# A four-layer graph network on one core: a fourth pair list with six passes behind it, and three smaller edits

## The reference, cut to what matters

```python
def step(f, _):                       # second layer, K = 10, ALPHA = 0.1
    msg = f[src] * edge_weight[:, None]
    agg = segment_sum(msg, dst, num_segments=n)
    return 0.9 * agg + 0.1 * feat_0, None
x = layernorm(x + relu_sum_layer(x, edge_attr, src, dst, eps))      # layer 0
x = layernorm(x + scan(step, x, length=10))                         # layer 1
x = layernorm(x + typed_mlp_layer(x, edge_weight1, w1, w2, src, dst, edge_type))   # layer 2
x = layernorm(x + segment_max_layer(x, theta, phi, src, dst))       # layer 3
```

## Time and profile before

| | |
|---|---|
| median of three runs | 4459.67 us |
| profiled execution, own time | 4465.7 us |
| its span | 4463.9 us |
| mean granted TensorE clock | 0.744 |
| VectorE busy | 2971.8 us (67%) |
| GpSimd busy | 2610.8 us (58%) |
| TensorE busy | 2502.3 us (56%) |

### The profile page before, as it was taken

How to read it: one execution, slowest core, us unless ns; L and a number is a source line. 1 busy time by engine, 2 the same in 40 slices (tenths; PEclk the granted TensorE clock), 3 DMA queues, 4 the chain that set the end, 5 groups by cost and what they waited for, 6 DMA issues and landing times. The chain is left out here.

```text
span 4463.9 us, 60648 instructions
## 1 busy us (share of the span) xinstructions
PE 2502.3 (56%) x9482; PEld 1176.3 (26%) x9482; DVE 2971.8 (67%) x7710; ACT 1232.9 (28%) x3893; POOL 2610.8 (58%) x2544
## 2 busy tenths in 40 slices
PE   4720000677777588888888487561222104995654
PEld 2510000333333244344444222111111101333332
DVE  7989997988888488788888586332332234663333
ACT  0023332332232255445554222111000012441111
POOL 4747772655554477764444564774565613656776
PEclk9965555887777799899999799785555557995555
DMA  6647776888887866675555476333434243332111
GB/s 223 229 119 211 219 217 182 154 152 147 149 149 133 153 173 162 164 164 145 142 142 133 120 208 171 71 57 59 49 49 45 34 99 84 73 68 40 36 37 27
DMA packets 628412, 557.12 MB, mean 125 GB/s; under 512 B 379089, under 2 KB 548122, under 8 KB 623330
## 3 DMA queue, kind: packets, MB, share of 16 engines
q1 hardware_dynamic: 477606, 418.72, 34.7%
q0 software_dynamic: 90112, 95.44, 16.7%
q10 hardware_dynamic: 60612, 42.15, 3.5%
HBM read 291.63 MB, written 290.82 MB: 130 GB/s over the span
## 5 line engine op out<-in xcount | busy, mean ns | idle before, releaser
L1302 POOL DMA_INDIRECT out<-xob,ob x400 | 412.0, 1030 | 358.7 <-DVE xob L1414 251.8
L278 POOL DMA_INDIRECT gb<-nodes,ib x400 | 396.5, 991 | 348.9 <-ACT ib L855 249.6
L491 POOL DMA_INDIRECT xdst<-in_x,dstc x400 | 457.0, 1142 | 226.4 <-issue 135.1
L262 PE MATMUL bank<-ident,act 128*99 128x128 f32 x400 | 84.6, 348 | 666.2 <-DVE act L999 649.4
L298 PE MATMUL bank<-chosen,rec 128*6 128x512 bf16 x1200 | 370.0, 473 | 0.9 <-DVE chosen L285 0.9
L278 POOL DMA_INDIRECT cgb<-layer,ib x160 | 175.6, 1098 | 232.3 <-ACT ib L2193 185.9
L1341 PE MATMUL bank<-hm,w 128*48 128x512 f32 x600 | 296.0, 632 | 0.0
L1358 PE MATMUL bank<-bxT,w 105*128 105x512 f32 x600 | 283.2, 608 | 8.7 <-ACT bxT L1245 8.6
L272 PE MATMUL bank<-ident,scan 99*128 99x99 f32 (+2 forms) x1120 | 199.5, 308 | 152.1 <-DVE scan L2012 101.5
L291 PE MATMUL bank<-l_chosen,l_rec 128*3 128x512 f32 x480 | 250.6, 672 | 0.3 <-DVE l_chosen L285 0.3
L278 POOL DMA_INDIRECT parent<-upper_rows,ib x176 | 176.1, 1000 | 119.1 <-ACT ib L1270 54.6
(11 more groups left out here) (292 smaller groups left out, 6764.8 us busy)
## 6 DMA issues: line engine op xcount, KB each, us to landing
nodes<-wt SPq DMA_DIRECT2D x40, 1286.2 KB
edges<-gb ACTq DMA_DIRECT2D x100, 194.0 KB, 5.9
upper_rows<-tb SPq DMA_DIRECT2D x100, 194.0 KB, 4.9
xa<-upper_rows SPq DMA_DIRECT2D x100, 194.0 KB, 3.0
lsb<-edges SPq DMA_DIRECT2D x100, 194.0 KB
run_rows<-upper_rows SPq DMA_DIRECT2D x100, 194.0 KB, 4.3
deep_sum<-zeros SPq DMA_DIRECT2D x20, 960.0 KB, 21.6
layer<-zeros SPq DMA_DIRECT2D x20, 960.0 KB, 25.1
```

The costliest lines, as they stand in the source:

```text
L262: last = nc.tensor.transpose(slot(dst_ps[0:w, :], t), rows_sb[:, t, c0:c0 + w], ident[:, :])
L278: yield nc.gpsimd.indirect_dma_start(out=dst[s][:, t, 0:width], out_offset=None, in_=table, in_offset=bass.IndirectOffsetOnAxis(ap=ib[s][: ...
L491: nc.gpsimd.indirect_dma_start(out=xdst[:, k * F:(k + 1) * F], out_offset=None, in_=a["x"], in_offset=bass.IndirectOffsetOnAxis(ap=dstc[:, ...
L1302: nc.gpsimd.indirect_dma_start(out=out, out_offset=bass.IndirectOffsetOnAxis(ap=ob[s][:, t:t + 1], axis=0), in_=xo[s][:, t, :], in_offset= ...
```

## The change

`LU` becomes `(4, 4, 2, 2)`, there are 19 rows of `lists`, a third `deep_sum` table and a fourth `list_keep`. Level 2 now also packs a list and scatters its sums, as level 1 does; a new level 3 on the new list does what level 2 did; and `steps` runs on the new list with six passes instead of seven. The norm of list 0 adds the third table. In counting, `hot_no` becomes four 16-bit `tensor_scalar` comparisons, and ScalarE makes one of eight `hot_at` tiles. In the first edge stage the 99 keep rows come from one 1 KB load and one bf16 product of 3 rows, copied by ScalarE from PSUM. The `deep_sum` and `layer` tables are cleared in the second edge stage.

```diff
-LU = (4, 4, 2)
+LU = (4, 4, 2, 2)
...
                 def mark(i, b):                                # counting, ScalarE
+                    nc.scalar.copy(lines[b][:, :], col(line_no, g)).then_inc(s_mark, 1)
                     nc.scalar.copy(marks[b][:, :], col(line_at, g)).then_inc(s_mark, 1)
+                    if b == 1:
+                        nc.scalar.mul(away[:, :], col(line_at, g)[:, T - 1:T], -1.0).then_inc(s_away, 1)
+                        act.wait_ge(s_away, 2 * i + 1)
+                        nc.scalar.activation(gap[:, :], steps_h[:, :], ACT.Abs, bias=away[:, 0:1], scale=1.0).then_inc(s_away, 1)
+                        wait(act, s_count, g - 1)
+                        act.wait_ge(s_away, 2 * i + 2)
+                        nc.scalar.activation(hot_at[b][:, T - 1, :], gap[:, :], ACT.Relu, bias=one[:, 0:1], scale=-1.0).then_inc(s_near, 1)
...
                 def compare(i, b):                             # counting, VectorE
-                    nc.vector.tensor_tensor(hot_no[b][:, :, :], steps_h[:, 0:P]..., col(line_no, g)..., ALU.is_equal)
-                    dve.wait_ge(s_mark, g + 1)
+                    dve.wait_ge(s_mark, 2 * g + 2)
                     for t in range(T):
+                        nc.vector.tensor_scalar(hot_no[b][:, t, :], steps_h[:, 0:P], lines[b][:, t:t + 1], None, ALU.is_equal)
+                    for t in range(T - b):
                         last = nc.vector.tensor_scalar(hot_at[b][:, t, :], steps_h[:, :], marks[b][:, t:t + 1], None, ALU.is_equal)
...
-                for z in (*deep_sum, *layer.values()):         # counting, SP
-                    for j in range(EP * F // P // ZW):
-                        sp.dma_start(zr[:, j * ZW:(j + 1) * ZW], zeros[:, :]).then_inc(s_clear, 16)
...
                 def load(i, s):                                # first edge stage, SP
-                    wait(sp, s_scan, g - U + 1)
-                    sp.dma_start(kb[s][0:2 * F, :], edge_keep[0:1, bass.ds(g * GE, GE)].to_broadcast([2 * F, GE]))
-                    sp.dma_start(kb[s][2 * F:PW, :], edge_keep[0:1, bass.ds(g * GE, GE)])
+                    wait(sp, s_spread, g - U + 1)
+                    sp.dma_start(keeps[s][0:1, :], keep_half[0:1, bass.ds(g * GE, GE)]).then_inc(s_kb[s], 16)
...
+                def copy_keeps(i, s):                          # ScalarE, first in its body, ahead of relued
+                    act.wait_ge(s_spread, g + 1)
+                    wait(act, s_scan, g - U + 1)
+                    nc.scalar.copy(kb[s][:, :], psK[b][0:MW, :]).then_inc(s_kept, 1)
...
+                def spread_keeps(i, s):                        # TensorE, first in its body, ahead of columns
+                    pe.wait_ge(s_kb[s], (i + 1) * 16)
+                    wait(pe, s_kept, g - 1)
+                    nc.tensor.matmul(psK[b][0:MW, :], pick[:, :], keeps[s][:, :], start=True, stop=True).then_inc(s_spread, 1)
...
+                def clear_sums(i, s):                          # second edge stage, SP, listed turns
+                    for z in deep_sum:
+                        sp.dma_start(rows(z, part_of(i) * U + s, 1), blank[:, :]).then_inc(s_blank[s], 16)
+                def clear_layers(i, s):                        # second edge stage, SP, every group
+                    for z in layer.values():
+                        sp.dma_start(rows(z, i * U + s), blank[:, :]).then_inc(s_fresh[s], 16)
...
     level(1, level_rows[0])
     prepare(2, 12, 14)
-    first_rows("deep", (level_rows[2],), (idx3, oi2, w_2))
-    level(2, level_rows[1])
+    level(2, level_rows[1])                                    # with pack_up and scatter to deep_sum[1]
+    prepare(3, 16, 18)
+    first_rows("deep", (level_rows[3],), (idx3, oi2, w_2))
+    level(3, level_rows[2])
...
     one(0, level_rows[3], swap_rows, "first")                  # powers
     one(1, swap_rows, level_rows[3], "add")
-    with eng.Fori(1, (STEPS - 4) // 2) as j:
-        one(j * 2, level_rows[2], swap_rows, "add")
-        one(j * 2 + 1, swap_rows, level_rows[2], "add")
-    one(STEPS - 4, level_rows[2], None, "end")
+    one(2, level_rows[3], swap_rows, "add")
+    one(3, swap_rows, level_rows[3], "add")
+    one(4, level_rows[3], swap_rows, "add")
+    one(STEPS - 5, swap_rows, None, "end")
...
                     sp.dma_start(flat(d1[s]), rows(deep_sum[1], g, 1)).then_inc(s_in[s], 16)   # norm of list 0
+                    sp.dma_start(flat(d2[s]), rows(deep_sum[2], g, 1)).then_inc(s_in[s], 16)
...
+                    nc.vector.tensor_tensor(d1[s][:, :, :], d1[s][:, :, :], d2[s][:, :, :], ALU.add).then_inc(s_add, 1)
```

More of the change, by code:

```diff
@@ L140, in gnn @@
         first_sum = dram("first_sum", (EP, F))
-        deep_sum = [dram(f"deep_sum{k}", (EP + 1, F)) for k in range(2)]
+        deep_sum = [dram(f"deep_sum{k}", (EP + 1, F)) for k in range(3)]
         layer = {k: dram(f"layer{k}", (OFF + EP + 1, F)) for k in (2, 3)}
-        lists = dram("lists", (15, LW))
+        lists = dram("lists", (LISTS, LW))
         onehot = dram("onehot", (R + 1, EP))
@@ L177, in gnn @@
         iota_h = sb("iota_h", [P, GE], F16)
-        count = [sb(f"count{k}", [1, 1], I32) for k in range(3)]
+        count = [sb(f"count{k}", [1, 1], I32) for k in range(4)]
         count_b = sb("count_b", [1, 1], I32)
@@ L501, in gnn @@
             hot_at = [sc(f"hot_at{b}", [P, T, LINE], F16) for b in range(2)]
-            marks = [sc(f"marks{b}", [P, T]) for b in range(2)]
+            marks, lines = ([sc(f"{n}{b}", [P, T]) for b in range(2)] for n in ("marks", "lines"))
+            away, one, gap = sc("away", [P, 1]), sc("one", [P, 1]), sc("gap", [P, LINE], F16)
+            s_away, s_near, s_one = scope.sem("h_away"), scope.sem("h_near"), scope.sem("h_one")
             run_end_c = sc("run_end_c", [P, NG * T])
@@ L960, in _ @@
                     last.then_inc(s_zero, 1)
+                    dve.wait_ge(s_kt, 16 * 2)
+                    nc.vector.tensor_copy(pick[:, :], pick3[:, :])
+                    for z in keeps:
+                        last = nc.vector.tensor_copy(z[:, :], tail3[:, :])
+                    last.then_inc(s_kp, 1)
                     def run_end(i, s):
@@ L1124, in gnn @@
             first_list = preparation(0, scope)
+            blank = scope.enter_context(nc.sbuf_tensor("blank", [P, T * F], F32))
+            s_blank, s_fresh = ([scope.sem(f"b_{n}{s}") for s in range(U)] for n in ("blank", "fresh"))
             s_count = first_list[3][3]
@@ L1198, in store_parents @@
                         sp.dma_start(rows(parent_rows, part_of(i) * U + s), flat(parent[s])).then_inc(s_pw[s], 16)
+                    def clear_sums(i, s):
[4 more added lines that the diff above has]
+                            sp.dma_start(rows(z, i * U + s), blank[:, :]).then_inc(s_fresh[s], 16)
                     def rest_of_parents(m):
+                        for s in range(U):
+                            sp.wait_ge(s_fresh[s], 16 * NT * len(layer))
+                            sp.wait_ge(s_blank[s], (m + 1) * 16 * len(deep_sum))
+                        sp.sem_inc(sp_turn, 1)
                         for s in range(U):
```

138 lines of the change are left out of this document (77 added, 61 removed).

## The result

Without the change the kernel takes 4459.67 us, with it 4405.71 us: a ratio of 0.9876, 95% interval 0.9848 to 0.9905. (Of three executions of the changed kernel one, at 6345.85 us, was disturbed and is left out; the other two took 4405.71 and 4404.40 us.) The profiled execution has a span of 4403.9 us where the one before had 4463.9, 60.0 less; the prediction said 81.7 less. So it was faster, inside the range, 28 us above the forecast: 22 from the terms, and 6 since this profiled execution is itself the median, where the one before lay 6 above.

A forecast was written before the change was run, and what follows sets the result against it. VectorE was taken to bound counting and the first edge stage, VectorE and TensorE evenly the second, POOL the rest from level 1. Terms of -204, +114, +15, -11, +1, -10, +14 gave 81.7 us less: 4378 us, range 4325 to 4435.

The forecast's parts named there:

- Passes: Last stage: six passes over 6 groups instead of seven over 10, 204 us less.
- lists: Pair lists: level 2 packs and scatters, a new level 3 and one more `prepare`, 114 us more.
- norm: Norm of list 0: a fourth load and a third addition per group, 15 us more.
- The 13 us of standstill stay: Between passes: POOL stands still 13.0 us while last stores land, unchanged with fewer groups.
- the ring of the third rival: Level 2: two slots and TensorE at 1.2 GHz make a group 13 us, not 10.2; 4406 us, chance 0.10.
- Counting: Counting stage: four short comparisons lose 0.06 us a group, ScalarE's `hot_at` share gains 0.17; 11 us less.
- TensorE's 1.54 us per group stay below the new 1.84: Counting stage: TensorE's 1.54 us per group remain shorter than VectorE's new 1.84 us.
- First edge stage: First edge stage: VectorE's work unchanged, shorter TensorE idling keeps its clock higher; 10 us less.
- When TensorE runs at 2.4 GHz they fall into the 2.39 us in which it waits for `act`, and cost nothing: First edge stage: new product and ScalarE copy fit TensorE's 2.39 us wait at 2.4 GHz, at no cost.
- The slower rival: First edge stage: TensorE always at 1.2 GHz, a serial chain of 8.5 us per group instead of 6.8; 4558, chance 0.03.
- The rival of the clock: First edge stage: the clock stays up, giving the whole 40 us instead of 10; 4348 us, chance 0.24.
- Second edge stage: Second edge stage: clears mostly covered by SP's 2.8 us wait per group; start and traffic cost 14 us more.

The follow-up runs named there:

- run 10: Changed kernel with four groups instead of six in the last list's level and the passes, two turns written out: 4295.82 us, ratio 0.9631 to the kernel before.
- run 11: Changed kernel with the same six groups, but the three turns written out without the loop: 4398.74 us, ratio 0.9859 to the kernel before.
- Run 6: Changed kernel with four instead of two buffers in the counting stage: 4417.57 us, ratio 0.99 to the kernel before.
- run 7: Changed kernel with four counting buffers and 104 instead of 128 early gathers, the other 24 moved into the node stage: 4391.84 us, ratio 0.9845.
- run 4: Changed kernel with the tables cleared in the counting stage again and no clears in the second edge stage: 4389.15 us, ratio 0.9846.
- run 3: Changed kernel with the counting stage as in the kernel before: 4410.52 us, ratio 0.9884.
- run 12: Changed kernel with keep-row product and copy one group ahead, clears in counting, four counting buffers and 104 early gathers: 4360.7 us, ratio 0.9763.

## Why the prediction came out right, and where it was wrong

**Passes, lists, norm** were right within 4 us each, and by their own working: groups times GpSimd's 1.25 and 1.29 us a gather and a scatter, plus parts that don't depend on groups. "The 13 us of standstill stay" held, at 12.7 to 13.3 us, though runs 10 and 11 show that 3.6 of them belonged to groups past the list's end, a part that does depend on how many groups there are. It was there before and after, so the sum did not suffer. The passes written out cost nothing that shows (43.1 us each, where 43.6 was worked out). Level 2 took 126.8 us where 123.3 was worked out; the ring of the third rival, at 150, did not come about.

**Counting**: the step that failed is that "TensorE's 1.54 us per group stay below the new 1.84". Taken by itself it is true, and the durations were right too (four short steps of 0.165 us, `hot_at` 0.34). But a buffer of two comes back only after TensorE has picked up, worked and answered, some 1.9 us, which holds the short groups at 1.90 us where VectorE needs 1.71. Run 6 removed that and got the 11 us back in the stage itself. What the prediction did not ask at all is how VectorE's new stream of short steps slows GpSimd's gathers beside it; runs 6 and 7 show that this decides what the stage is worth.

**First edge stage**, the largest miss (25 us): the step that failed is "When TensorE runs at 2.4 GHz they fall into the 2.39 us in which it waits for `act`, and cost nothing". TensorE waited for `act`, so what delays `act` is not hidden by that wait. The product can't use that wait: it stands behind the sums of the group before, and ScalarE's Relu stands behind the copy of the product. The slower rival named the right chain, at one tenth of its price: the clock did not fall to 1.2 GHz in every group.

The rival of the clock was half right. The granted clock from 800 to 1400 us was 0.81 with the product, and 0.75 to 0.79 with the old loads. The Trainium skill (TensorE: Matmul & The Clock Gate, Part 1) has it that activity releases the clock; the traces agree in the direction. But the clock never came near the 0.90 of the early stretch, and the stage gave none of the 10 us back: with the chain through ScalarE longer, three groups of four packed at a partly lower clock, where it had been every second. The stage was short, 662.3 us at a clock of 0.84, only with the product and its copy ahead. How much of that is the clock and how much the shorter chain no run separates.

**Second edge stage**: 7 us instead of 14, inside its bounds. SyncE's 2.8 us of waiting for parents did cover the clears: that wait, 79.6 us in the earlier trace rows, is not among SyncE's waits after the change. The cost is the head alone, 6 us by run 4; the 14 us stood for the start and the traffic of the clears together, and behind the head no trace shows any.

The terms were 22 us too hopeful in sum, nearly all of it counting and the first edge stage (11 and 25), less what the second edge stage and the node stage gave back (7 and 6). The node stage's part is luck, since no term stood for it. The large terms, which carried the 60 us, were each within 4%.

## What to carry to other kernels

Ask of an operation that is added on an idle engine not whether the engine has room, but what it is queued behind there and what is queued behind it: in an in-order queue a product of 0.41 us and a copy of 0.59 us a group, on two engines with room, cost 10 us in a stage, and the same work one group ahead took 17 us off it. Two buffers are enough only while the consumer's whole round trip, pickup and answer with it, is shorter than the producer's step; shorten the producer and they become the bound. Before a wait is taken from one engine, look at what another one sends beside it: here comparisons that ended 11 us sooner made the next stage start 16 us later, through GpSimd. Rounding a short list up to whole turns costs more than its idle groups' share, where what they fetch lands late.

## What the runs showed of the hardware

What VectorE executes sets the pace of GpSimd's indirect gathers, though in this stage no gather waits for VectorE in the program. They start each 1.25 us where VectorE is idle or in a scan (run 6, from 247 us). They start each 1.32 us beside an unbroken stream with a `TENSOR_TENSOR` in each group (before, and run 3), each 1.31 beside 16-bit `TENSOR_SCALAR` steps with a pause of 0.14 us in every second group (after), each 1.87 beside the same steps without a pause (runs 6, 7 and 12), and each 3.51 beside f32 `TENSOR_TENSOR` and `CAST` of 2000 numbers in turn (run 6, from 240 us). The Trainium skill (SBUF — State Buffer, "Who interferes with whom") says that the two engines lock a pair of ports against each other while VectorE runs in a two-port mode. The traces agree so far as the gathers themselves grow longer (0.95 us alone, 1.40 and 1.74 in turn in run 6) and keep step with VectorE's instructions. Which instructions hold them, and that it is this lock, was not tested by itself.

Gathers of groups past a list's end landed late in the passes: 4.2 to 8.1 us from the start of the group's last gather to its message, where others took 2.7 to 4.0, over all traces. That the cause is the index, which is the same in all their rows, is argued from the list's length; no run gave those groups other indices.
